# Four spill semaphores, two buffers of decay steps, and two order tables for the filling units of a linear-attention layer

## The reference

```
x = x + 0.5 * ffn(layernorm(x))      # 8 experts, 2 of them per token, 256 -> 896 -> 256
x = x + attention(layernorm(x))
x = x + 0.5 * ffn(layernorm(x))
```

```
state = state * exp(g_t)
delta = (v_t - k_t @ state) * beta_t
state = state + outer(k_t, delta)
out_t = q_t @ state
```

## Time and profile before

| what | value |
|---|---|
| median of 3 runs | 2986.46 us (2980.61 to 2987.47) |
| the profiled execution | 2988.33 us, of which the profile's span is 2986.1 us |
| PE busy | 2701.9 us, 90% of the span |
| DVE busy | 1930.2 us, 65% |
| ACT busy | 1397.8 us, 47% |
| POOL busy | 678.0 us, 23% |

### The profile page before, as it was taken

The page is one execution under the profiler, slowest core; times in us unless marked ns, Lnnn a source line. Parts: engine busy times, 40 slices in busy tenths (PEclk is TensorE's granted clock), DMA queues, the critical chain, the costliest instruction groups (busy, mean ns, idle before and its releaser), DMA issues. The chain is left out here.

```text
span 2986.1 us, 58338 instructions
## 1 busy us (share of the span) xinstructions
PE 2701.9 (90%) x19346; PEld 1997.4 (67%) x19347; DVE 1930.2 (65%) x3648; ACT 1397.8 (47%) x4441; POOL 678.0 (23%) x938
## 2 busy tenths in 40 slices
PE   4899995556999999999999999999999995799996
PEld 4566663333677777777777777777777774566664
DVE  5122222588999999999999999999987544322221
ACT  0111111333667667666666766766765551111111
POOL 0222221222222221221222222222221101122221
PEclk7999997777999999999999999999999996799998
DMA  4133312244645545545555545545543313132322
GB/s 160 45 79 102 96 28 53 73 140 146 199 150 188 161 148 185 163 148 183 168 145 180 172 147 174 176 148 169 177 144 95 104 54 119 31 96 65 100 61 46
DMA packets 378124, 374.74 MB, mean 125 GB/s; under 512 B 213076, under 2 KB 293460, under 8 KB 377876
## 3 DMA queue, kind: packets, MB, share of 16 engines
q1 hardware_dynamic: 362900, 351.05, 37.3%
q0 software_dynamic: 14976, 20.46, 4.1%
HBM read 234.83 MB, written 138.67 MB: 125 GB/s over the span
## 5 line engine op out<-in xcount | busy, mean ns | idle before, releaser
L533 PE MATMUL f_ps_up<-f_wbuf,f_xgT 128*128 x1248 | 500.3, 544 | 5.1 <-issue 3.2
L628 DVE TENSOR_TENSOR f_h<-f_h,f_ps_up 128x448 f32<-128x448 f32 x156 | 96.9, 621 | 472.2 <-ACT f_h L602 472.2
L602 ACT ACTIVATE f_h<-f_ps_up 128x448 f32<-128x448 f32 x156 | 85.0, 545 | 635.9 <-PE f_ps_up L533 635.9
L533 PEld LDWEIGHTS f_ps_up<-f_wbuf,f_xgT 128*128 128x128 f32 x1248 | 231.6, 192 | 189.7 <-issue 185.1
L1270 PE MATMUL at_bank<-xnT,at_w_qk 128*128 128x512 f32 x512 | 273.2, 662 | 58.9 <-DVE at_qk L1597 55.5
L1597 DVE SCALAR_TENSOR_TENSOR at_qk<-at_bank,at_taps_qk,at_qk 128x510 f32<-128x510 f32 (+2 forms) x384 | 281.9, 744 | 64.9 <-ACT at_qk L1468 55.5
L1597 DVE SCALAR_TENSOR_TENSOR at_vT<-at_bank,at_taps_v,at_vT 128x510 f32<-128x510 f32 (+2 forms) x384 | 280.4, 744 | 36.5 <-ACT at_vT L1475 27.5
L1846 POOL TENSOR_SCALAR at_small<-at_small 128x4 f32<-128x4 f32 x64 | 17.3, 270 | 1154.6 <-ACT at_squares L1502 1154.6
L500 POOL DMA_INDIRECT sums<-f_y,f_row_of x78 | 123.9, 1589 | 582.7 <-DVE f_y L639 582.7
L555 PE MATMUL f_ps_y<-f_wbuf,f_hT 128*128 x1092 | 248.8, 379 | 1.6 <-DVE f_hT L632 1.6
L1295 PE MATMUL at_bank<-at_w_vz,xnT 128*128 128x256 f32 x1024 | 243.6, 381 | 7.0 <-DVE at_vT L1597 6.9
(11 more groups left out here) (232 smaller groups left out, 5657.4 us busy)
## 6 DMA issues: line engine op xcount, KB each, us to landing
f_wbuf<-in_L_ffn_w_dram SPq DMA_DIRECT2D x48, 896.0 KB, 6.8
at_steps_e<-steps_kept SPq DMA_DIRECT2D x64, 512.0 KB, 6.7
pt_kept<-at_pt_made SPq DMA_DIRECT2D x64, 512.0 KB, 2.7
mt_kept<-at_mt_made SPq DMA_DIRECT2D x64, 512.0 KB, 4.1
at_mt<-mt_kept SPq DMA_DIRECT2D x64, 512.0 KB, 4.0
at_pt<-pt_kept SPq DMA_DIRECT2D x64, 512.0 KB, 4.5
qk_kept<-at_qk SPq DMA_DIRECT2D x64, 256.0 KB, 2.7
ks_kept<-at_ks_made SPq DMA_DIRECT2D x64, 256.0 KB, 2.7
```

Source lines behind the costliest of these rows:

```text
L533: last = te.matmul(ps_up[hf][w][:, 0:MH], xgT[b][:, k, :], wbuf[:, bass.ds(off + (w * WSIZE + k * M + hf * MH), MH)], start=(k == 0), stop ...
L628: v.tensor_tensor(part, part, ps_up[hf][1][:, 0:MH], ALU.mult).then_inc(h_ready, 1)
```

## The change

Four things change, all in the attention layer.

1. Each of the four spills becomes a step of its own with its own pair of semaphores (`qk_spilled`, `ks_spilled`, `pt_spilled`, `mt_spilled`), and each waiter waits for its own spill alone.
2. `steps_e` has two buffers, `load_steps` moves from stage 11 to stage 12, and waits for the scan of two units ago. The room comes from `squares`, whose user `turn` now writes into the scratch tile `junk` (shared with `norm`, so each of the two waits for the other's last use), and from the table `b`, which now lies in the table `g`.
3. The filling rounds are parted: rounds -12 to -7 follow new tables (`FRONT_...`), rounds -6 to -2 new ones too (`FILL_...`). Steady and draining tables stay, with the four spills in the place of the one.
4. `seen`, which told PE how many times another step was issued, now counts in a `Counter` what `walk` has issued; `proj_qk` waits for `v_free` as well.

The core of the diff (of the ten new tables, only a few lines of two):

```diff
-    "load_steps": 11, "turn": 11, "ks": 11, "scales": 11, "diag": 11, "products": 11, "scan": 11, "mix": 11,
-    "spill": 11,
+    "load_qk": 12, "load_steps": 12, "proj_qk": 12, "conv_qk": 12, "gate_qk": 12,
+    "spill_qk": 11, "spill_ks": 11, "spill_pt": 11, "spill_mt": 11,
...
+FRONT_PE_ORDER = (("y_turn", 0), ("solve", 0), ("state",), ("proj_v", 2), ("inv_x", 64), ("turn", 1), ("project", 0),
+                  ("turn", 0), ("inv_x", 32), ("solve", 1), ("proj_qk", 0), ("turns", 0), ("turns", 1), ("inv_n",),
...
+FILL_SP_ORDER = (("blocks_in",), ("spill_qk",), ("load_c",), ("load_steps",), ("store_up",), ("store_low",),
+                 ("load_qk",), ("spill_ks",), ("load_vz",), ("spill_mt",), ("load_wo",), ("load_t",), ("spill_pt",),
...
+def phase_of(i):
+    if i < -STAGE["blocks"]:
+        return "front"
+    if i < -STAGE["proj_v"]:
+        return "fill"
+    return "steady" if i < UNITS + FIRST else "drain"
...
-        squares = r.sb("squares", [P, Q4, P])
-        steps_e = r.sb("steps_e", [P, N8 * P])
+        steps_e = [r.sb(f"steps_e{k}", [P, N8 * P]) for k in range(2)]
...
-                    at_least(sp, s["decay_ready"], idx(u))
+                    at_least(sp, s["decay_ready"], idx(u) - 1)
...
-                        sp.wait_ge(s["spilled"][k], SPILL * (2 * u[0] + 2))
+                        sp.wait_ge(s["mt_spilled"][k], 16 * (2 * u[0] + 2))
...
-                    at_least(act, s["spilled"][two(u)], SPILL * (of_two(u) - 1))
+                    at_least(act, s["qk_spilled"][two(u)], 16 * (of_two(u) - 1))
...
-                    at_least(act, s["spilled"][1 - two(u)], SPILL * of_two(shift(u, -1)))
+                    at_least(act, s["ks_spilled"][1 - two(u)], 16 * of_two(shift(u, -1)))
...
-                    at_least(dve, s["spilled"][1 - two(u)], SPILL * of_two(shift(u, -1)))
+                    at_least(dve, s["pt_spilled" if of else "mt_spilled"][1 - two(u)], 16 * of_two(shift(u, -1)))
...
+                    at_least(pe, s["v_free"], 2 * seen(("proj_v", 2 + ct)) - 1 + ct)
```

More of the change, by code:

```diff
@@ L1 @@
+from collections import Counter
 from contextlib import ExitStack
@@ L904 @@
 STAGE = {
-    "load_qk": 12, "proj_qk": 12, "conv_qk": 12, "gate_qk": 12,
-    "load_steps": 11, "turn": 11, "ks": 11, "scales": 11, "diag": 11, "products": 11, "scan": 11, "mix": 11,
-    "spill": 11,
+    "load_qk": 12, "load_steps": 12, "proj_qk": 12, "conv_qk": 12, "gate_qk": 12,
+    "turn": 11, "ks": 11, "scales": 11, "diag": 11, "products": 11, "scan": 11, "mix": 11,
+    "spill_qk": 11, "spill_ks": 11, "spill_pt": 11, "spill_mt": 11,
     "blocks_in": 7,
@@ L921 @@
 FIRST, AFTER = -max(STAGE.values()), -min(STAGE.values())
[L923 to L936, removed]
@@ new lines @@
+FRONT_ACT_ORDER = (("inv_n",), ("turn", 1), ("turn_copies", 0), ("turn", 0), ("conv_v", 2), ("z_gate", 0),
+                   ("y_copy", 0), ("norm",), ("inv_last",), ("copy_state",), ("conv_v", 3), ("z_gate", 1),
+                   ("weigh", 0), ("y_copy", 1), ("conv_qk", 0), ("conv_qk", 1), ("from_state",), ("gate_qk", 0),
+                   ("weigh", 1), ("gate_v", 2), ("ks",), ("gate_qk", 1), ("turn_copies", 1), ("lift",), ("gate_v", 3))
+FRONT_DVE_ORDER = (("blocks", 0), ("blocks", 1), ("inv_x", 64), ("inv_x", 32), ("add", 0), ("conv_qk", 0),
+                   ("conv_qk", 1), ("join",), ("blocks", 2), ("scan",), ("from_state",), ("shape",), ("mix", 0),
+                   ("add", 1), ("conv_v", 2), ("conv_v", 3), ("blocks", 3), ("mix", 1))
@@ new lines @@
+FILL_ACT_ORDER = (("y_copy", 0), ("gate_v", 2), ("turn", 1), ("z_gate", 0), ("inv_n",), ("lift",), ("z_gate", 1),
+                  ("weigh", 0), ("turn", 0), ("conv_qk", 0), ("from_state",), ("conv_qk", 1), ("turn_copies", 0),
+                  ("conv_v", 2), ("gate_v", 3), ("gate_qk", 0), ("turn_copies", 1), ("y_copy", 1), ("conv_v", 3),
+                  ("gate_qk", 1), ("norm",), ("inv_last",), ("copy_state",), ("ks",), ("weigh", 1))
+FILL_DVE_ORDER = (("conv_v", 2), ("add", 0), ("conv_qk", 0), ("shape",), ("blocks", 0), ("conv_v", 3), ("conv_qk", 1),
+                  ("blocks", 1), ("inv_x", 64), ("blocks", 2), ("scan",), ("join",), ("from_state",), ("add", 1),
+                  ("blocks", 3), ("mix", 0), ("mix", 1), ("inv_x", 32))
@@ L1118, in walk @@
         def walk(orders, steps):
-            filling, steady, draining = orders
+            issued.clear()
             for i in range(FIRST, UNITS + AFTER):
-                for name, *args in filling if i < -STAGE["proj_v"] else steady if i < UNITS + FIRST else draining:
+                for name, *args in orders[phase_of(i)]:
                     u = shift((i // BP, i % BP), STAGE[name])
@@ L1501, in turn @@
                     for t in range(Q4):
[L1502 removed]
+                        last = sc.activation(junk[:, Q4 * (1 - a) + t, :], src[:, P * t:P * t + P], ACT.Square,
                                              accum_out=small[two(u)][:, 4 * a + t:4 * a + t + 1])
```

132 lines of the change are left out of this document (79 added, 53 removed).

## The result

The changed kernel takes 2958.59 us (median of 4 runs, 2956.76 to 2958.83), the kernel before, beside it, 2986.75: a ratio of 0.9909, 95% interval 0.9892 to 0.9926, a gain of 0.9%, and the interval does not reach 1. The forecast was 2959.0 us, between 2947 and 2974.

The account below looks back on a forecast made before the run. PE bounds the steady half, a chain through engines the first filling rounds, DVE rounds -6 to -2. Savings 0.5 + 17.8 + 9.2 + 0 = 27.5 us take 2988.33 to 2960.8 profiled, 2959 as median; range 2947 to 2974.

Parts of the forecast that it names:

- Rounds -10 to -7: Filling rounds: each falls from 14.65 to 10.2 us, saving 17.8 us (14.2 to 21.5).
- three loops: Candidates to close a round of -10 to -7: DVE's work 9.27 us, PE's loop 11.1, POOL's 9.0 to 9.9.
- The 10.2: Forecast length in us of a round from -10 to -7, the middle between 9.27 and 11.1.
- The loop by POOL: Rounds -10 to -7: SiLU, transposes to scales, scaled keys, handovers; 9.0 us, 9.9 with slow transposes.
- Round -11: First filling rounds: no `mt` to wait for, convolution at most 1 us earlier; 0.5 us saved.
- Rounds -6 to -2: Later filling rounds: DVE's 11.16 us of waits fall to 2, saving 9.2 us (7.6 to 11.2).
- The wait at `w_up`: DVE's 7.29 us wait for a store in rounds -6 to -2; 0 to 1 us remains with earlier issue.
- The head: Start of the steady rounds: later `load_t` costs 1 us, copies no longer waiting for `mt` give 1; sum 0.
- The decay steps count nothing: Filling rounds: loading them a round ahead hides a load that never stopped the scan; 0 us.
- Slower: Rival: `proj_qk`'s new wait for `v_free` holds PE in steady rounds; a 1 us loss each gives 3012; chance 0.04.
- nothing: Rival: steady rounds wait for something the filling rounds do not hurry, gain given back; 2978 to 2990 us; chance 0.06.
- PE stays fast: Rival: upper clock in the first rounds, round 9.27 us, 33.7 us saved, 2953; chance 0.20.

Follow-up runs that it names:

- e4: Changed kernel with SP issuing the stores of w_up and w_low behind the late spills again in rounds -6 to -2; 2959.24 us.
- e6: e5 with ACT doing the second SiLU ahead of the scaled keys in the first six rounds; 2954.74 us.
- e9: Changed kernel with the old order tables of SP, ACT, DVE and POOL in the first six rounds, PE's new one kept; 2965.03 us.
- e3: Changed kernel with the decay steps' load issued in the round of its scan again, not a round ahead; 2958.79 us.
- e5: Changed kernel with the first half's projection moved ahead of the transposes in PE's order of the first six rounds; 2950.96 us.
- e11: Changed kernel plus, in the first six rounds except for the first unit, a discarded extra projection at the head of PE's order; 2947.69 us.

## Why the prediction was right

*Rounds -10 to -7: 16.6 us instead of 17.8.* Of the three loops PE's did close the round, but by another link than the one priced. The forecast took all eight projection matmuls and the taps of the second half; with the 6.22 us that PE needed this loop comes to 0.63 + 6.22 + 0.63 + 2.27 + 0.3 = 10.05. The loop that closed runs through the first half's projection and the taps of both halves: 4.53 + 0.63 + 4.53 (582.39 to 586.92) + 0.69 and 0.13 between them, 10.5. I had priced that loop for round -6 alone. The 10.2 was a middle between DVE's 9.27 and PE's loop with a slow start, 11.1, and no row fixed the clock there. It did lie in between (transposes and projections 6.2 us; the sum had 4.96 and 7.23 as its ends), but the same order also ran two rounds of 9.02 (e4); that the middle came within 0.3 us is in part luck. The loop by POOL ended 0.56 us earlier, ACT's idle time before the SiLU at 581.70. One detail was wrong: I let POOL's loop set what the scaled keys' place is worth, and overlooked that PE's transposes wait for them (e6, e9). DVE's own round is 9.02, not 9.27: its instructions overlap a little.

*Round -11: 0.5 us, as forecast.* Its convolution starts 566.63 - 556.22 = 10.41 us behind that of round -12, before 567.04 - 556.12 = 10.92.

*Rounds -6 to -2: 10.6 us instead of 9.2.* Forecast were 2 us of waiting left; 1.29 are, all in round -6, inside its range of 0 to 2.6. The wait at `w_up` went wholly. The remaining 0.6 is busy time of DVE, 76.14 against 76.78.

*The head: 1.3 us gained instead of 0.* `load_t` came later, as said: `inv_n` starts 699.74 - 696.65 = 3.09 us behind the start of the round, before 724.75 - 724.18 = 0.57, so 2.5 us later, the end of what was allowed. DVE did not wait for what `inv_n` gives, so the priced 1 us was not lost, and DVE's waits for the copies of rounds -1 to 1, 0.9 us, were gained. Round 2 starts 28.8 us earlier, at 764.77 instead of 793.55. Another 0.7 came up to the end. These are one execution of each kernel, and what lies behind round -1 varies by more than that.

*The sum.* 2959.0 against 2958.59 is closer than its parts: they were off by -1.2, 0, +1.4, +1.3 and +0.7 us, and some of it cancels.

*The decay steps count nothing:* right in the time, wrong in the reason. The load had never stopped the scan in rounds of 14.65 us; in rounds of 10.5 it does when it is issued late (e3), and costs next to nothing there only because PE's loop is longer still.

*The rivals.* "Slower" and "nothing" did not show: the steady stretch kept its 1493 busy us and PE shows no wait for `v_free` at the projection. "PE stays fast" came in part of an execution (e4) and, once the gap is filled, in all rounds from -11 to -7 (e5, e11). They take 2951 and 2948 us against its 2953, although the wait of round -6 stays in both (1.38 and 1.39 us).

## What to carry to other kernels

A finer wait and a new order can be worth little or less than nothing apart and a lot together: before splitting a change into parts, ask which wait each order leans on. In a short loop that runs round through several engines, price the matmuls at the clock they get behind their idle time; a projection moved into the gap, or even one thrown away, can shorten the round. When one wait goes, list what is late next: here a load that had never mattered would have been late.

## What the runs showed of the hardware

More work on PE made the loop faster: four discarded matmuls a round raised the granted clock from 0.84 to 1.00 and took 1.48 us off each round (e11). With 2.5 to 2.7 us of idle time in a round of 9 to 10.5 us, both clocks occurred in the same execution with the same order; what tips it from the one to the other in e4 at about 588 us these runs do not show.
